# Delta rule chunk operands and products laid key-major, with the four steps innermost

## The reference

```python
def step(S, inp):
    kt, qt, vt, bt = inp
    err = jnp.einsum('bhvk,bhk->bhv', S, kt) - vt
    S = S - bt[..., None, None] * err[..., None] * kt[..., None, :]
    o = jnp.einsum('bhvk,bhk->bhv', S, qt)
    return (S, o)
...
q, k = _l2norm(q), _l2norm(k)          # after a causal convolution and two silu
beta = jax.nn.sigmoid(h @ Wbeta.T)
o, memory_state = _delta_scan(k, q, v, beta)
```

## Time and profile before

| | |
|---|---|
| median of 3 runs | 1543.97 us (1537.77 to 1548.41) |
| the profiled execution | 1549.48 us |
| its span in the trace | 1547.7 us |
| TensorE busy | 1138.0 us, 74% |
| VectorE busy | 969.1 us, 63%, 2520 instructions |
| ScalarE busy | 477.7 us, 31% |
| GpSimd busy | 172.7 us, 11% |
| mean granted TensorE clock | 0.82 |

### The profile page before, as it was taken

The page is one execution under the profiler, slowest core; times in us unless marked ns, Lnnn a source line. Parts: engine busy times, 40 slices in busy tenths (PEclk is TensorE's granted clock), DMA queues, the critical chain, the costliest instruction groups (busy, mean ns, idle before and its releaser), DMA issues.

```text
span 1547.7 us, 22181 instructions
## 1 busy us (share of the span) xinstructions
PE 1138.0 (74%) x8568; PEld 752.1 (49%) x8568; DVE 969.1 (63%) x2520; ACT 477.7 (31%) x995; POOL 172.7 (11%) x251
## 2 busy tenths in 40 slices
PE   5378547878877777878877887878887887777037
PEld 3146414555546544665445553655445554565025
DVE  3421376866777576865677575865777576846941
ACT  1024402434323412443332422433333422342011
POOL 2000000400031000400030010400030000400300
PEclk8579757979879887899878887989878887999559
DMA  9430413042211413041211414051301403001000
GB/s 294 40 33 5 55 62 33 2 61 67 31 18 36 50 56 33 2 70 56 35 14 40 54 47 33 1 69 58 40 9 41 64 30 33 1 14 61 0 14 7
DMA packets 112426, 64.76 MB, mean 42 GB/s; under 512 B 49184, under 2 KB 106688, under 8 KB 112320
## 3 DMA queue, kind: packets, MB, share of 16 engines
q1 hardware_dynamic: 109264, 58.19, 22.2%
q10 hardware_dynamic: 3056, 5.15, 1.2%
HBM read 45.73 MB, written 17.17 MB: 41 GB/s over the span
## 4 chain that ended last, share of the span: by engine, by line
PE 45%; DVE 25%; DMA 9%; SPq 7%; ACT 7%; issue 7%; POOL 1%; DVEq 0%; POOLq 0%; ACTq 0%
PE bank L1415 8%; PE bank L1395 5%; PE bank L1400 4%; DMA k_stack<-k_pieces 4%; PE bank L1334 4%; DVE k_l L1112 3%; PE bank L1553 3%; PE bank L1504 3%; DVE lane_buf L327 3%; PE bank L1326 2%; PE bank L1372 2%; PE bank L1576 2%; DVE lane_buf L1082 2%; DMA q_stack<-m_rows 2%; DVE conv L973 2%
## 5 line engine op out<-in xcount | busy, mean ns | idle before, releaser
L649 ACT ACTIVATE probs<-bank 128x512 f32<-128x512 f32 x256 | 149.2, 599 | 164.5 <-PE bank L1400 164.2
L903 DVE TENSOR_REDUCE mx<-bank 128x2 f32<-128x320 f32 x256 | 123.4, 491 | 84.1 <-PE bank L1372 75.2
L1415 PE MATMUL bank<-probs,v_ext 128*16 128x128 f32 x2048 | 160.8, 283 | 15.7 <-ACT probs L649 14.7
L1367 PE MATMUL bank<-edge_mask,identb 128*128 128x64 bf16 x512 | 70.0, 227 | 100.8 <-DMA k_stack<-k_pieces 43.3
L327 POOL TENSOR_TENSOR lane_buf<-state,q_l 128x128 f32<-128x128 f32 x128 | 87.8, 715 | 486.6 <-DVEq L1107 486.6
L1395 PE MATMUL bank<-tri_mask,identb 128*128 128x512 bf16 x256 | 112.8, 441 | 30.2 <-DMA q_stack<-m_rows 30.2
L1082 DVE TENSOR_TENSOR lane_buf<-state,til 128x128 f32<-128x128 f32 x256 | 104.1, 407 | 19.4 <-POOL lane_buf L537 10.1
L1367 PEld LDWEIGHTS bank<-edge_mask,identb 128*128 128x128 bf16 x512 | 35.2, 109 | 160.3 <-DVE mx L903 71.4
L1400 PE MATMUL bank<-q_stack,k_stack 128*128 128x128 bf16 x1024 | 112.4, 239 | 0.0
L1415 PEld LDWEIGHTS bank<-probs,v_ext 128*16 128x16 f32 x2048 | 87.0, 98 | 49.5 <-ACT probs L649 26.1
L1400 PEld LDWEIGHTS bank<-q_stack,k_stack 128*128 128x128 bf16 x1024 | 89.3, 108 | 39.7 <-issue 16.3
(11 more groups left out here) (156 smaller groups left out, 1918.7 us busy)
## 6 DMA issues: line engine op xcount, KB each, us to landing
k_stack<-k_pieces SPq DMA_DIRECT2D x192, 64.0 KB
q_stack<-q_pieces SPq DMA_DIRECT2D x192, 32.0 KB
q_l<-lane_q SPq DMA_DIRECT2D x8, 512.0 KB, 4.0
k_l<-lane_k SPq DMA_DIRECT2D x8, 512.0 KB, 4.7
q_pieces<-conv SPq DMA_DIRECT2D x24, 128.0 KB, 2.1
k_pieces<-conv SPq DMA_DIRECT2D x48, 64.0 KB, 2.0
x<-in_x SPq DMA_DIRECT2D x8, 256.0 KB, 2.8
x_in<-in_x SPq DMA_DIRECT2D x8, 256.0 KB, 8.5
```

The lines of the kernel that those rows point to most:

```text
L649: act.activation(probs[:, u % 3], score_bank[u % 3][:], ACT.Exp, scale=float(DK) ** -0.5).then_inc(exp_done, 1)
L903: dve.tensor_reduce(mx[:, g, 2 * v:2 * v + 2], bank[1 + u % 2][:, 0:2 * SPAN].rearrange("p (h k) -> p h k", h=2), AX.X, ALU.max).then_inc( ...
L1367: pe.matmul(edges[:, :, e * W:e * W + SUB], identb[:], edge_mask[:, e * SUB:(e + 1) * SUB].rearrange("p (o s) -> p o s", o=1) .broadcast_t ...
L1415: last = pe.matmul(bank[5][row:row + VE, col:col + W], v_ext[:, b, kb, h, :], probs[:, u % 3, (hp * 2 + kb) * W:(hp * 2 + kb + 1) * W], st ...
```

## The change

`til` and `first` are laid with the step index innermost instead of the key index: `til` goes from `[chunk, step, column]` to `[chunk, column, step]`, `first` from `[chunk, v, step, slot]` to `[chunk, v, slot, step]`. Sizes stay. All views of both are rewritten to match, so no instruction is added or removed: the copy on GpSimd, the two of `til_first`, the six of `til_column`, and L1082 and L1089 of each chunk walk their operands in another order. `beta_of` multiplies by minus one in the instruction that adds one, so that `beta_l` holds minus beta after the reciprocal; `til_first` and `pair_scale` then need no factor of their own and use a plain product of two tensors.

```diff
-        til = sb("til", [128, NC_, C, KV])
+        til = sb("til", [128, NC_, KV, C])
-        first = lane_buf[:].rearrange("p (c v i k) -> p c v i k", v=VR, i=C, k=DK + 1)
+        first = lane_buf[:].rearrange("p (c v k i) -> p c v k i", v=VR, i=C, k=DK + 1)
...
-                pool.tensor_copy(first[:, :, :, :, DK], til[:, :, :, DK:KV].rearrange("p c i v -> p c v i")
+                pool.tensor_copy(first[:, :, :, DK, :], til[:, :, DK:KV, :]
...
-                done(dve.tensor_scalar(beta_l[:], beta_l[:], 1.0, None, ALU.add))
+                done(dve.tensor_scalar(beta_l[:], beta_l[:], 1.0, -1.0, ALU.add, ALU.mult))
...
-                    last = dve.scalar_tensor_tensor(
-                        out=til[:, :, :, lo:lo + width].rearrange("p c i k -> p k (c i)"), in0=src[:], scalar=-1.0,
-                        in1=beta_l[:].rearrange("p (o t) -> p o t", o=1).broadcast_to([128, width, W]),
-                        op0=ALU.mult, op1=ALU.mult)
+                    last = dve.tensor_tensor(
+                        til[:, :, lo:lo + width, :].rearrange("p c k i -> p k c i"),
+                        src[:].rearrange("p k (c i) -> p k c i", i=C),
+                        beta_l[:].rearrange("p (o c i) -> p o c i", o=1, i=C).broadcast_to([128, width, NC_, C]),
+                        ALU.mult)
...
-                    last = dve.scalar_tensor_tensor(out=pair_l[:, at:at + m, :], in0=pair_l[:, at:at + m, :], scalar=-1.0,
-                                                    in1=bc[:, j + 1:C], op0=ALU.mult, op1=ALU.mult)
+                    last = dve.tensor_tensor(pair_l[:, at:at + m, :], pair_l[:, at:at + m, :], bc[:, j + 1:C], ALU.mult)
...
-                done(dve.tensor_tensor(tmp_til[:, :, 0:m], g, til[:, :, j:j + 1].broadcast_to([128, NC_, m, KV]), ALU.mult))
-                last = dve.tensor_tensor(til[:, :, j + 1:C], til[:, :, j + 1:C], tmp_til[:, :, 0:m], ALU.add)
+                ti = til[:].rearrange("p c k i -> p c i k")
+                done(dve.tensor_tensor(tmp_til[:, :, 0:m], g, ti[:, :, j:j + 1].broadcast_to([128, NC_, m, KV]), ALU.mult))
+                last = dve.tensor_tensor(ti[:, :, j + 1:C], ti[:, :, j + 1:C], tmp_til[:, :, 0:m], ALU.add)
...
-                        first[:, c, :, :, 0:DK],
-                        state[:, c, :, :, C].rearrange("p v (o k) -> p v o k", o=1).broadcast_to([128, VR, C, DK]),
-                        til[:, c:c + 1, :, 0:DK].broadcast_to([128, VR, C, DK]), ALU.mult))
+                        first[:, c, :, 0:DK, :],
+                        state[:, c, :, :, C:C + 1].broadcast_to([128, VR, DK, C]),
+                        til[:, c:c + 1, 0:DK, :].broadcast_to([128, VR, DK, C]), ALU.mult))
...
-                    at = mark(dve.tensor_reduce(u_l[:, c], first[:, c], AX.X, ALU.add))
+                    at = mark(dve.tensor_reduce(u_l[:, c], first[:, c].rearrange("p v k i -> p v i k"), AX.X, ALU.add))
```

## The result

The changed kernel takes 1566.12 us (median of 4 runs, 1565.35 to 1568.08) against 1541.83 for the kernel before in the same session: ratio 1.0155, 95% interval 1.0116 to 1.0195. It is slower, by more than the 1% that tells a change from none. In a later session it took 1568.02 against 1547.80 (ratio 1.0139, 1.0091 to 1.0188). The runs of the kernel before scatter more than its first three showed: 1536 to 1561 us over all sessions. So a single difference of medians is good to some 4 to 8 us (half the width of the intervals), and the parts of the traces say more.

The account below looks back on a forecast made before the run. Neither TensorE nor VectorE bounds throughout; VectorE sets the time in five of eight preparations. Preparations 10.5 plus 66 chunks 0.7 give +11.2 us on 1544.0, so 1555; range 1542 to 1568.

Parts of the forecast that it names:

- the fourth rival: Scan's product with the state: gains nothing because the state still jumps 20 bytes every fourth element; +18.7 us, 1563; chance 0.07.
- the third: Column sums of `til_column`: pay for strided read and strided write; preparation grows by 3.50, +23.7 us, 1568; chance 0.12.
- only the sum is free: Rival for L1089: its strided single source costs nothing where products pay; preparation +1.60, total +2.9 us, 1547; chance 0.13.
- nothing costs: Rival: 16-byte strides cost nothing in the changed instructions; preparation shorter by 1.63 us, total -11.5, 1532.5; chance 0.10.
- L1082 wins nothing: Rival for the scan's product: no 88 ns gain per chunk, as the state still jumps; +18.7 us, 1563; chance 0.07.
- The filling: `til_first` in the preparation: its two instructions get runs of four, -752 and -379 ns, together -1.13 us a tile.
- The columns: `til_column` in the preparation: products and sums become strided, 4608 elements at 0.70 ns, +3.23 us a tile, ends +2.12 and +3.41.
- pays twice: Rival for `til`'s sum: strided read and write both cost, adding 1.61 us per preparation; +23.7 us, 1568; chance 0.12.
- The preparation: `til_first`, `pair_scale`, `til_column`, GpSimd's copy, chunks 0 to 2: +1.89 us, passing whole in five tiles, 10.5 together.
- The cover: VectorE's waits for TensorE ahead of `result` in three tiles, 2.03, 0.87 and 2.15 us, swallow part of the longer preparation.
- The last scan: Last tile, no TensorE instruction: 29 chunks count in full at 0.011 us each; as long as before within 1 us.
- The count of chunks: Chunks counted outside the preparation: 16 between maxima, 21 ahead of first residuals, 29 in the last tile; 66 x 0.011 = 0.7 us.

## Why the prediction held, and where it was off

The sign, the range and the reason held: the time of 1566 lies in the range, above the point of 1555, and the change lost in the columns of `til` more than it won in the filling. The size was off, +11.2 forecast, +20 and +24 measured. That is more than the sum's own bounds, +3 to +14. The range held the time only because it was drawn wide enough for the rivals and for the spread of the runs, and that part is luck; the later 1568.02 would have touched its end. By the time alone the fourth rival (1563) or the third (1568) would have looked best, and the rows refute both. By its steps:

- **L1082, L1089.** Forecast -88 and +99, measured -91 and +111 as means; medians 384 to 293 and 303 to 411, so -91 and +108. The chunk is 0.02 us longer without GpSimd, 0.01 forecast. A sum pays for a stride like a product does: the rivals "only the sum is free", "nothing costs" and "L1082 wins nothing" fall. The rule of the Trainium skill that I cited from its page "SBUF — State Buffer", section "Door 1: The DMA port swizzle", is borne out here in three points: the sum pays, the state's jump every fourth element of the product doesn't (L1083 has a median of 293 ns, as L1095 has), and two hits in a line are enough (959 ns at 768 elements in runs of two).
- **The filling.** Forecast -1.13 us, measured -0.75 and -0.37: -1.12.
- **The columns.** The term that was mis-sized. Forecast +3.23 us (0.70 ns per element), measured 2258 + 1543 + 846 + 2273 + 1555 + 863 ns against 2 x (1358 + 958 + 557): +3.59, 0.78 per element. I had taken a mean of rows at 16 and 48 bytes; the value nearest in length, 0.73 and 0.74, would have been closer, and all lie under it. The sum has two strided streams and costs no more than the product, 2273 against 2258: the rival "pays twice" falls.
- **GpSimd's copy.** Forecast -0.24, measured -0.50, at the bound of 0.47 from its contiguous copies; the figure that I cited from the Trainium skill, page "GPSIMD Engine Reference", section "Performance pitfalls for Q7 kernels", would have given -0.38 as an estimate. Here the rows at hand beat it.
- **The preparation.** Forecast +1.89, measured +2.18 (17.4 over eight).
- **The cover.** I let TensorE swallow 4.7 us (0.87 and twice 1.89), from one trace; the two traces of before have 11.5 and 9.0 us in the waits behind the preparations and the changed kernel 6.6, so 4.9 and 2.4 went, 3.6 in the mean. 17.4 less 3.6 is 13.8, against 10.5 forecast. Which tiles have the cover changes from run to run (2.03 us at 738 in one trace, elsewhere in the other), and so does its sum: ahead of `result` VectorE waited 5.1 us for TensorE in the first trace and 2.7 in the second. One trace was too little to take it from.
- **The last scan.** Forecast +0.3 us, measured +2.43, of which 1.97 is the meeting with GpSimd. That step failed: I costed the scan's instructions alone on their engine, though the earlier trace rows showed a maximum of 849 ns and the mean of L1082 lay 23 ns over its median, both the sign of the same thing before. 22 stretched products of before became 51.
- **The count of chunks.** The 66 take 16 between maxima; seven tiles have a scan beside an attention, so it is 14, and 64 in all. That changes the sum by 0.02 us.
- **What stays open.** 13.8 + 2.4 is 16.2, of 20 and 24 by the medians; the intervals (+14 to +29 us and +18 to +30) hold it or nearly so. In the traces the attention parts are 7 us longer than in the two of before, the middle parts 4 shorter and the start ahead of the first preparation 2.5 longer. Between the two traces of before these differ by 5.8, 3.9 and 1.8, and over all thirteen traces the attention parts lie between 555.5 and 568.0 with no order by layout (564.0 in the kernel before without the terms). So the rest is no more than scatter as far as these traces go, and a cause for it isn't shown. It is not the meeting with GpSimd in the other seven tiles, which VectorE's waits for TensorE hide.

## What to carry to other kernels

A product that contracts over one axis and its successor over another can't both have their axis innermost; relaying the tiles moves the price from the product to the sum, and then the passes that fill the tile decide, since they are the long ones. Before choosing a layout, list every instruction that walks the tile with its innermost run: two floats in a row are enough, one isn't. And where a stretch of work ends together with another engine's, a loss counts nearly in full and a gain much less: of +17.4 us in the preparations 13.8 were left behind the waits, of -6.7 us only 1.9. And where one engine's instructions stretch another's, they should be costed together if the stretched one sets the time; where it waits anyway, 20 us of stretch cost nothing that could be measured.

## What the runs showed of the hardware

- VectorE, float32: 0.61 to 0.78 ns more per element in instructions of 128 elements and more as soon as an operand stands 16, 20 or 48 bytes apart, read or written, in products and in sums. Two strided streams cost no more than one: 2273 ns with read and write, 2258 with one read, 1359 with none, at 1152 elements. Runs of 2 and of 3 floats in 16 bytes are free: 959 against 958 ns at 768 elements, 1359 against 1357 at 1152.
- GpSimd, float32 copy of 512: 1111 ns with both sides strided, 1100 with the destination alone, 1074 with the source alone, 613 with runs of four on both.
- ScalarE's copy of 512 floats out of PSUM: 585 ns contiguous, 1018 when it writes 64 bytes apart.
- A two-source product of VectorE, 128 elements, that begins while GpSimd runs a product of its own ends as if held until 0.147 us before the end of GpSimd's: 0.80 us for 0.29 when both begin together, 0.59 at 0.21 us behind, 0.39 at 0.41, 0.29 in the last 0.15 us (200 products in the two traces of the changed kernel, to 13 ns). Without GpSimd's terms none of the changed kernel's is over 0.303 us, and one-source sums are hardly touched (L1090 at most 429 ns).
- With the new durations the two engines fall into step: two chunks of 1.97 and 1.52 us last as long as one group of five GpSimd instructions, 3.50 us, and each group catches another product. They find this step again when GpSimd starts 0.10 us later; why they do isn't shown.
